# Factor rows of the exponents taken through a DRAM scratch, the loop of passes written out, and new orders on every engine

## What is computed

```python
zxbcdt = xn @ W_in                       # z 512, xBC 768, dt 8 columns
dt = softplus(dt + dt_bias)
xBC = silu(causal_conv(xBC, conv_w, conv_b))       # 4 taps
x, B, C = split(xBC, [512, 640])
A_cum = cumsum(dt * a)                   # a = -exp(A_log), 8 heads
L = exp(A_cum[l] - A_cum[s]) for s <= l
Y_diag = einsum('ln,sn,hls,shp->lhp', C, B, L, x * dt)
Y_off  = C . state * exp(A_cum);  state carried from chunk to chunk
y = (Y_diag + Y_off + x * D) * silu(z)
y = y * rsqrt(mean(y * y) + EPS) * rms_w
out = layernorm(xn + y @ W_out) * ln_g + ln_b
result = x_in + out + tanh(xn @ F1 @ F2 @ F3 + f_bias)
```

## Time and profile before

| | |
|---|---|
| three timed runs | 766.77, 768.09, 768.17 us, median 768.09 |
| the profiled execution | 769.67 us, of which the span is 768.0 us |
| mean granted clock of TensorE | 0.981 |
| busy share of the span | PE 93%, DVE 89%, POOL 78%, ACT 76% |
| DMA issues for factors | 512 of 2 KB each (256 for `right`, 256 for `left`) |
| packets of the DMA queues | 60073, 38.35 MB, mean 50 GB/s |

### The profile page before, as it was taken

One profiled execution on the slowest core, in us unless ns is written; L12 is line 12 of the kernel. 1 busy time (PEld: TensorE's weight loads), 2 busy tenths in 40 slices (PEclk: granted clock), 3 DMA queues, 4 the chain that ended last, 5 costly groups with the idle time before them and its releaser, 6 DMA issues. The chain is left out here.

```text
span 768.0 us, 17761 instructions
## 1 busy us (share of the span) xinstructions
PE 712.0 (93%) x4728; PEld 574.9 (75%) x4728; DVE 686.3 (89%) x1321; ACT 580.4 (76%) x1425; POOL 597.5 (78%) x932
## 2 busy tenths in 40 slices
PE   5979999999999989998999989999999999999983
PEld 4767777787778677786887768777787878877763
DVE  3779999898989879898998989989899999989884
ACT  3787878877797777876878678787878778787851
POOL 2538798787978769886897968879787888979773
PEclk7999999999999999999999999999999999999996
DMA  6001310211212021120211212011121202011110
GB/s 214 2 4 32 97 56 18 85 31 31 70 46 71 19 65 48 30 69 19 82 31 30 69 46 68 18 58 55 31 71 45 72 18 72 16 32 56 32 56 29
DMA packets 60073, 38.35 MB, mean 50 GB/s; under 512 B 7120, under 2 KB 59472, under 8 KB 59984
## 3 DMA queue, kind: packets, MB, share of 16 engines
q1 hardware_dynamic: 58768, 37.40, 16.0%
q10 hardware_dynamic: 1216, 0.02, 0.1%
HBM read 27.70 MB, written 8.65 MB: 47 GB/s over the span
## 5 line engine op out<-in xcount | busy, mean ns | idle before, releaser
L2626 PE MATMUL ring<-xhl,wh 128*128 128x512 f32 x620 | 207.8, 416 | 1.4 <-DVE xs L1136 1.2
L1136 DVE SCALAR_TENSOR_TENSOR xs<-ring,cw,xs 128x512 f32<-128x512 f32 x273 | 196.6, 738 | 6.3 <-issue 5.0
L2626 PEld LDWEIGHTS ring<-xhl,wh 128*128 128x128 f32 x620 | 107.5, 189 | 33.1 <-issue 11.2
L2157 ACT ACTIVATE xdt<-xt_bank,dts 128x64 f32<-128x64 f32 x512 | 111.8, 334 | 13.8 <-PE xt_bank L2712 13.5
L2626 PE MATMUL ring<-xhl,wl 128*128 128x512 f32 x310 | 122.0, 394 | 0.0
L634 POOL TENSOR_TENSOR lay<-lay,xd 128x512 f32<-128x512 f32 x62 | 79.9, 1288 | 31.3 <-DVE lay L1174 31.3
L2087 ACT ACTIVATE xs<-ring,cb,cw 128x512 f32<-128x512 f32 x91 | 71.9, 790 | 38.8 <-PE ring L2626 38.3
L1165 DVE SCALAR_TENSOR_TENSOR lay<-e_bank,btg 128x512 f32<-128x512 f32 x128 | 85.4, 678 | 0.0
L2137 ACT ACTIVATE e_bank<-e_bank 128x512 f32<-128x512 f32 x128 | 76.0, 605 | 7.5 <-PE e_bank L2742 7.3
L2626 PE MATMUL bg_bank<-woh,yts 128*128 128x256 f32 x252 | 74.9, 297 | 5.6 <-DVE hh L1239 4.3
L627 POOL TENSOR_TENSOR xd<-xs,d_ch 128x512 f32<-128x512 f32 x64 | 67.1, 1048 | 14.4 <-ACT xs L2102 13.2
(11 more groups left out here) (184 smaller groups left out, 1838.5 us busy)
## 6 DMA issues: line engine op xcount, KB each, us to landing
grow<-scratch SPq DMA_DIRECT2D x124, 128.0 KB, 3.0
xin<-in_x_dram SPq DMA_DIRECT2D x32, 256.0 KB, 2.8
out_dram<-res SPq DMA_DIRECT2D x31, 256.0 KB, 2.6
right<-rows SPq DMA_DIRECT2D x256, 2.0 KB
left<-rows SPq DMA_DIRECT2D x256, 2.0 KB
lay<-in_w_in_dram SPq DMA_DIRECT2D x1, 776.0 KB, 8.6
lay<-in_w_in_dram SPq DMA_DIRECT2D x1, 512.0 KB, 10.2
sq<-in_w_out_dram SPq DMA_DIRECT2D x1, 512.0 KB, 5.4
```

The costliest lines, as they stand in the source:

```text
L1136: v.scalar_tensor_tensor(out=to, in0=conv_bank(j, ct), scalar=cw[:, ct, t:t + 1], in1=to, op0=ALU.mult, op1=ALU.add).then_inc(tap_done[ct], 1)
L2157: last = s.activation(xdt[:, q, head], xt_bank[:, head], ACT.Copy, scale=dts[:, b, at:at + 1])
L2626: last = mul(out, a, c, start=first and i == 0, stop=i == n - 1)
```

## The change

Three things are changed; what is computed and the shapes of all instructions on PE, DVE, ACT and POOL stay.

1. **Factors.** SP first writes the rows of both chunks to a new DRAM tensor `factors` (two DMAs of 16 partitions by 2 rows), and `growth` behind them; all three count in one semaphore, `rows_put`. The factors of a chunk are then read back with three DMAs: one for `right` (8 partitions by 4 heads, without zeros between heads) and two for `left` (4 partitions by 4 groups each). The waits of PE and ACT on `factors_in` count 48 a step in place of 256.
2. **The loop.** `Fori` becomes a Python `for`, so passes 4 to 11 stand in the program one behind the other.
3. **Orders.** Head, pass and tail have new lists on all five engines, and the cut between passes lies elsewhere (SP's pass begins with `put_rows(j - 1)`). The sums of squares are folded with the same strided read as before.

```diff
--- before.py
+++ after.py
@@
+        factors = nc.dram_tensor("factors", (BUF, C, 2, Q * H, P), F32, kind="Internal").ap()
@@ def passes
-            with eng.Fori(first // BUF, last // BUF) as i:
+            for i in range(first // BUF, last // BUF):
@@ SyncE
-            def put_growth(j, b):
+            def put_rows(j, b):
                 sp.wait_ge(sums_read, j + 1)
+                apart(sp)
+                sp.wait_ge(rows_done, j + 1)
                 apart(sp)
                 if begun(j - BUF):
                     for q in range(Q):
                         sp.wait_ge(grow_loaded[q], 32 * (C * (j - 1) - 1))
                         apart(sp)
-                sp.dma_start(scratch[b], growth[:, :]).then_inc(growth_put, 16)
+                    for c in range(C):
+                        sp.wait_ge(factors_in[c], 48 * (j - 1))
+                        apart(sp)
+                for c in range(C):
+                    sp.dma_start(factors[b, c].rearrange("l n t -> n l t"), rows[c * Q * H:(c + 1) * Q * H, b].bitcast(F32)).then_inc(rows_put, 16)
+                sp.dma_start(scratch[b], growth[:, :]).then_inc(rows_put, 16)
@@ def spread_factors(j, b, c):
-                sp.wait_ge(rows_done, j + 1)
+                sp.wait_ge(rows_put, 48 * (j + 1))
...
-                for i in range(FOUR):
-                    for low in range(2):
-                        at, n = c * Q * H, 2 * FOUR * i + FOUR * low
-                        sp.dma_start(right[n:n + FOUR, c, i].bitcast(F32), rows[at + i:at + Q * H:FOUR, b, low].bitcast(F32)).then_inc(factors_in[c], 16)
-                        sp.dma_start(left[LO + n:LO + n + FOUR, c, i].bitcast(F32),
-                                     rows[at + FOUR * i:at + FOUR * (i + 1), b, low].bitcast(F32))\
-                            .then_inc(factors_in[c], 16)
+                sp.dma_start(right[0:2 * FOUR, c].bitcast(F32), factors[b, c].rearrange("l (g i) t -> (l g) i t", i=FOUR))\
+                    .then_inc(factors_in[c], 16)
+                for low in range(2):
+                    at = LO + FOUR * low
+                    sp.dma_start(left[at:at + FOUR, c].bitcast(F32), factors[b, c, low].rearrange("(g i) t -> i g t", i=FOUR))\
+                        .then_inc(factors_in[c], 16)
@@ def spread_growth(j, b, c, q):
-                sp.wait_ge(growth_put, 16 * (j + 1))
+                sp.wait_ge(rows_put, 48 * (j + 1))
@@ SyncE, def one_pass(j, b, b1):
+                put_rows(j - 1, b1)
+                spread_factors(j - 1, b1, 0)
+                load_again(j + 1, b1, 0)
+                load_again(j + 1, b1, 1)
+                spread_growth(j - 1, b1, 0, 1)
                 spread_growth(j - 1, b1, 0, 0)
-                spread_growth(j - 1, b1, 0, 1)
                 spread_factors(j - 1, b1, 1)
                 spread_growth(j - 1, b1, 1, 0)
                 store(j - 2, b, 0)
+                store(j - 2, b, 1)
                 spread_growth(j - 1, b1, 1, 1)
-                store(j - 2, b, 1)
-                load_again(j + 2, b, 0)
-                load_again(j + 2, b, 1)
-                put_growth(j, b)
-                spread_factors(j, b, 0)
```

More of the change, by code:

```diff
@@ L1048, in tail @@
                 softplus(15, 1, 7)
+                scale_x(14, 0, 1, 0)
+                softplus(15, 1, 8)
                 rms_scale(14, 0, 0)
-                softplus(15, 1, 8)
                 softplus(15, 1, 9)
+                join_skip(14, 0, 1, 0)
                 softplus(15, 1, 10)
+                mask_g(14, 0, 1, 1)
                 softplus(15, 1, 11)
+                residual_bias(15, 1, 0)
+                residual(15, 1, 1)
+                skip_x(14, 0, 1, 1)
                 residual_bias(15, 1, 1)
@@ L1463, in head @@
                 tap(1, 1, 4, 2)
+                apply_gate(0, 0, 1, 0)
+                weigh(0, 0, 1, 1, 1)
+                scale_off(0, 0, 1, 1)
+                weigh(0, 0, 1, 1, 0)
                 tap(1, 1, 5, 0)
-                join_spill(1, 1, 0)
-                add_diag(0, 0, 1, 0)
+                y_low(0, 0, 1, 0)
                 tap(1, 1, 5, 1)
-                apply_gate(0, 0, 1, 0)
+                last_h(0, 0, 0, 1)
                 tap(1, 1, 5, 2)
-                scale_off(0, 0, 1, 1)
@@ L1471, in head @@
[L1471 removed]
+                last_stats(0, 0, 0, 0)
                 join_spill(1, 1, 2)
[L1473 to L1474 removed]
                 last_stats(0, 0, 0, 1)
[L1476 to L1477 removed]
+                last_mean_var(0, 0, 0, 0)
                 last_mean_var(0, 0, 0, 1)
[L1479 removed]
+                add_diag(0, 0, 1, 1)
+                new_state(0, 0, 1, 1)
@@ L1491, in head @@
                 last_h(0, 0, 1, 0)
+                last_stats(0, 0, 1, 0)
+                new_state(1, 1, 0, 0)
                 weigh(1, 1, 0, 0, 0)
+                last_h(0, 0, 1, 1)
                 weigh(1, 1, 0, 0, 1)
-                norm_stats(3, 1, 0)
-                last_h(0, 0, 1, 1)
-                last_stats(0, 0, 1, 0)
                 last_stats(0, 0, 1, 1)
-                add_diag(1, 1, 0, 0)
-                last_mean_var(0, 0, 1, 0)
+                scale_off(1, 1, 0, 1)
@@ L1607, in head @@
-                tap(3, 1, 1, 1)
-                apply_gate(2, 0, 1, 0)
-                join_spill(3, 1, 1)
-                mean_square(2, 0, 0)
-                tap(3, 1, 4, 0)
-                tap(3, 1, 1, 2)
-                tap(3, 1, 0, 0)
-                last_h(2, 0, 0, 0)
-            def tail():
+            def tail():
+                new_state(10, 0, 0, 1)
+                fold(10, 0, 0, 1)
+                softplus_rc(11, 1)
+                y_low(10, 0, 0, 1)
+                tap(11, 1, 3, 0)
+                scale_off(10, 0, 1, 0)
+                tap(11, 1, 3, 1)
+                mean_square(10, 0, 0)
+                tap(11, 1, 1, 0)
+                tap(11, 1, 3, 2)
+                tap(11, 1, 1, 1)
+                weigh(10, 0, 1, 0, 0)
+                weigh(10, 0, 1, 0, 1)
+                tap(11, 1, 4, 0)
+                join_spill(11, 1, 1)
+                tap(11, 1, 1, 2)
+                tap(11, 1, 0, 0)
+                last_h(10, 0, 0, 0)
+                add_diag(10, 0, 1, 0)
@@ L2924, in head @@
                 conv_project(1, 1, 2)
-                x_tokens(0, 0, 0, 1)
+                states(0, 0, 0, 0)
+                exponents(0, 0, 0, 1, 1)
+                y_diag(0, 0, 0, 0)
+                exponents(0, 0, 0, 1, 0)
+                x_tokens(0, 0, 1, 0)
                 branch_project(1, 1, 1, 1)
                 branch_project(1, 1, 1, 0)
-                exponents(0, 0, 0, 1, 1)
-                b_and_g(0, 0, 0, 1)
-                y_diag(0, 0, 0, 0)
-                states(0, 0, 0, 0)
@@ L2980, in head @@
-                y_off(1, 1, 0, 1)
-                exponents(1, 1, 0, 1, 1)
+                x_tokens(1, 1, 1, 0)
+                y_diag(1, 1, 0, 0)
+                conv_project(2, 0, 2)
+                branch_project(2, 0, 0, 0)
                 branch_project(2, 0, 0, 1)
-                branch_project(2, 0, 0, 0)
-                conv_project(2, 0, 2)
-                x_tokens(1, 1, 1, 0)
+                exponents(1, 1, 1, 0, 1)
+                b_and_g(1, 1, 1, 1)
+                states(1, 1, 0, 1)
```

1707 lines of the change are left out of this document (840 added, 867 removed).

## The result

| kernel | median, us | lowest to highest | ratio to before, 95% |
|---|---|---|---|
| before, beside it | 768.13 | 766.77 to 770.61 (4) | |
| changed | 748.09 | 746.41 to 750.24 (4) | 0.9737, 0.9701 to 0.9773 |

The change takes 20.0 us off. The forecast was 740.0 (729 to 757), so the sign and the range held and 8 us of the expected 28 are missing. The profiled execution of the changed kernel took 748.51 us, its span is 746.5.

What follows compares the result with a forecast made beforehand. DVE, with one stretch a pass decided by SP's issuing, was taken as the bound. Loop ends 10.7 us, passes 15.6 and the end about 1.0 plus 0.65 make 28.0 off 768.09: 740.1 us, forecast 740, range 729 to 757.

Steps and rivals of the forecast that it cites:

- Part 1: Hardware loop written out: three loop ends cost 4.5, 3.1 and 3.1 us, 10.7 us in all, and all should go.
- the clock's bill: Behind a loop end TensorE's clock was 0.50: 12 `out_project` matmuls took 2.5 us against 1.7, and `last_h` waited 1.84.
- The third turn: Price of the third loop end in the hardware loop, taken to be the second's, 3.1 us.
- the 108 ns for a branch: Trainium skill's compare-and-branch time; by it three loop ends would cost 0.3 us and the forecast be some 10 us higher.
- Part 2: Factors through DRAM end DVE's growth wait: 0.65 us off a 44.0 us pass, period 43.35; ends 0 and 1.3 us.
- The list of times: SP's DMA starts and landings after `low_rows` (R): needed growth lands R + 11.6 to R + 12.3, today about R + 14.5.
- next in line is `last_h`: DVE's next wait behind `scale_off`, for `out_project`: only 0.3 us gained there plus another 0.35, so 0.65 a pass.
- Part 3: New instruction orders, same work on each engine: booked at nothing; start bounded by -3 and +5 us, taken as 0.
- The cover I named: Chains followed through one pass come to their readers 0.5 to 1.2 us ahead of need.
- B: New wait replaces the old, through late loads of `x` or PE's chain taking the gain: period 44.0, 750 us; chance 0.22.
- A: DVE runs almost free: period 42.7, 731.5 us; chance 0.18.
- D: Slower: loads of `x` behind the round trip make DVE wait 3 us a pass, about 779 us; chance 0.05.

## Why the prediction came out as it did

**The accounting.** Of the 8.0 us between 740.1 and 748.09, 6.5 are in the span. From step 2 to step 15 it is 685.18 - 116.85 = 568.3 us, where 13 x 43.35 = 563.6 were forecast: +4.8, of which 3.1 is the one pass of 46.42 us and 1.7 the period of 43.49 in the other twelve. What follows the last `a_all` takes 61.3 instead of 57.8 us: +3.5. The head is 1.8 shorter. 4.8 + 3.5 - 1.8 = 6.5. The other 1.5 us lie in how the profiled executions stand to the medians (1.6 us above before, 0.4 after) and in 0.3 us around the span.

**Part 1, the loop: 10.7 us, measured 13.0 by itself.** The mechanism was right: nothing in the middle of the changed kernel has an "issue" gap of 2 us. What was read wrong is its make-up. DVE's gap at its own loop end was missed, and the clock's bill came at the first of the three loop ends only. Nor is it one number. By the passes the loop is worth 12.1 us in the old orders with direct copies, 13.6 with the DRAM transport and 1.2 in the new orders; by the medians 13.0, 16.9 and 5.3. The third turn, taken as 3.1 us, is 47.55 - 44.5 = 3.05.

The Trainium skill, "Runtime: NRT & Kernel Launch", Instruction fetch mechanics, says that a taken branch whose target is outside the two pages that an engine holds forces a fetch before execution goes on, while straight code is fetched ahead. The traces agree on both halves: gaps of 1.74 and 2.47 us at loop ends, with 9 packets of the instruction queues in such a pass against 2 in its neighbour, and no such gap in the written-out kernels. This is the rule I should have weighed beside the 108 ns for a branch. What the runs show besides is that the gap can be absent with the same loop, and that the instructions of straight code come in beside data loads, one of which then landed in 4.4 us.

**Part 2, the factors: 17.3 us (15.6 of passes, 1.65 at the end), measured 12.5 in the old orders.** This term was 4.8 us too large. The passes gave 11.1 us of the 15.6 (577.8 - 566.7), and the end gave 0.3 of the 1.65 (what follows the last `a_all` went from 59.4 to 59.1). The list of times held, and where it erred it was late: puts at R + 0.6, the third at R + 1.5, loads of factors from R + 3.2, SP free at R + 4.4 (forecast 5.4 to 6.0), growth loads from R + 5.7 (forecast about R + 7), `scale_off` at R + 15.3 without a wait, `last_h` with 0.37. The landing of the puts was 1.5 us on the page. The period was forecast as 43.35 and is 43.5. The reason given for it does not hold, though: DVE's list is not what then decides. A pass without `x` statistics was to be 1 us shorter and is not; DVE 2.6 us lighter gives 0.17. So the nearness of 43.35 is in good part luck: the limit that took over, PE's work or the hand-offs behind it, happens to lie there, and "next in line is `last_h`" caught it only in part.

**Part 3, the orders: booked at nothing, cost 5.5 us.** This is the step that failed most. Against the forecast's 10.7 + 17.3 + 0 = 28.0 us the runs give 13.0 + 12.5 - 5.5 = 20.0: Part 1 brought 2.3 more, Part 2 brought 4.8 less, and Part 3 cost 5.5. That the first two errors offset each other by half is luck. 742.6 with the old orders is 2.5 us above the forecast, 748.1 with the new ones 8.0. By the spans the two differ by 3.1 us: -0.7 in the head, +1.7 from step 2 to 15 and +2.2 behind the last `a_all`, where the new order leaves more matmuls of PE (314 against 296). The remaining 2.4 us are between how the two profiled executions stand to their medians: that of the old orders was the slowest of its four, at a granted clock of 0.982 against 0.985 to 0.987 in the others. The cover I named, the slack of 0.5 to 1.2 us at the chains, held in the steady pass: both have 43.5. It wasn't looked for in the head and in the tail. The +1.7 is one pass, the one from step 2 to 3, which takes 46.42 us in the new orders and 44.81 in the old ones with the same transport; the steady passes are alike. In this pass DVE's work counts: the run with lighter folds brings it to 44.92 us and the one with less PE leaves it at 46.45. In the kernel before it took 45.95 us, so the forecast, which used one period for all thirteen passes, was bound to be low there in any case.

**Rivals.** B's time (750) was nearest, and one of its two mechanisms, PE taking the place of DVE's wait, is part of the truth; its other one, the loads of `x` late, is not: they have about 3 us to spare (I gave 1.4 to 2.1). The forecast takes about 2 us for any DMA from the Trainium skill, "DMA: Bandwidth & Descriptors", Anatomy of one DMA; that section gives it for DMAs issued by GpSimd, while these are issued by SP, and the puts landed in 1.5 us. A is out: with DVE relieved by 2.6 us a pass the period was still 43.3. D's mechanism is real: it begins at about 2.7 us of delay, and it is the largest part of the 88 us that direct copies cost in the new orders; the change doesn't reach it.

## What to carry to other kernels

Before costing an edit on the busiest engine, ask whether a second engine stands within a microsecond of it and whether a stretch without some of that engine's work is any shorter: here one row, the pass without `x` statistics, tells it, and taking 1.85 us from an engine that was busy 99.8% of a pass gave back 0.4, and taking work off both engines is the test that tells it. A shift of instructions that costs nothing in the steady pass still has to be followed through the first and the last ones, and orders tuned for one transport are worth testing apart from it: the old orders with the new transport were the fastest kernel of this study. A loop end is a gap on each engine at its own cut, so its price has to be read at every cut and for the order at hand; 12 us of the passes here were 1 with other lists.

## What was unexpected in the hardware

- A loop end left a gap of 1.74 us on DVE and 2.47 us on ACT, at a granted clock of 1.00 and with no wait that the profile shows. In the new orders, with the same loop, neither gap appears.
- Issuing a DMA from SP costs by its form: 0.58 us for a factor copied within the on-chip memory, 0.28 us for `right<-factors` and 0.25 to 0.30 for one `left<-factors` out of DRAM. Two puts and six such loads replace 32 issues a step, so SP's time for the factors falls from 19.8 to 2.9 us (0.80 + 0.28 + 0.90 + 0.31 + 0.63).
- Taking 1.85 us of matmuls a pass away made the passes of a kernel 4.3 us longer in all. Four growth loads landed in 3.9 to 4.4 us instead of about 3, each while a packet of instructions came in, and DVE waited up to 3.2 us for them.
